# Eight last heads transposed by DMA, the last products one step later, and one low part moved ahead of the first rotation

## What is computed

```python
# part 1: x0 = x + einsum('bct,bcd->bdt', x, weights[subjects])      (32 x 32 weights per sequence)
# part 2: x0 + attention(x0)
q = rmsnorm(x0 @ Wq.T, q_norm_w)      # 32 heads of 128
k = rmsnorm(x0 @ Wk.T, k_norm_w)      # 8 heads of 128
v = x0 @ Wv.T                         # 8 heads of 128
q, k = rope(q, pos), rope(k, pos)
k_all = concat([k_cache[block_table], k])     # 16 pages of 32 keys, and 32 new keys
v_all = concat([v_cache[block_table], v])
scores = where(valid, q @ k_all * SCALE, -1e30)   # each key head serves four query heads
out = x0 + (softmax(scores) @ v_all) @ Wo.T
```

## Time and profile before

| | |
|---|---|
| median of three runs | 1012.82 us (1011.83 to 1014.14) |
| the profiled execution | 1012.16 us |
| its span, first to last instruction | 1010.1 us |
| busy: TensorE, VectorE, ScalarE, GpSimd | 96%, 81%, 73%, 54% |
| mean granted clock of TensorE | 0.997 |

### The profile page before, as it was taken

One profiled execution on the slowest core, in us unless ns is written; L12 is line 12 of the kernel. 1 busy time (PEld: TensorE's weight loads), 2 busy tenths in 40 slices (PEclk: granted clock), 3 DMA queues, 4 the chain that ended last, 5 costly groups with the idle time before them and its releaser, 6 DMA issues.

```text
span 1010.1 us, 24830 instructions
## 1 busy us (share of the span) xinstructions
PE 966.2 (96%) x8123; PEld 803.1 (80%) x8123; DVE 819.5 (81%) x1749; ACT 735.7 (73%) x2008; POOL 546.2 (54%) x715
## 2 busy tenths in 40 slices
PE   6899999999899999899999999999999999989998
PEld 4678888887677787688888888888888888878885
DVE  7789999999997689888877877777887787777770
ACT  5798999988774688777767767776776676766660
POOL 6565665565893068646644555454445545544540
PEclk9899999999999999999999999999999999999999
DMA  5799999989998989999999998998999998999940
GB/s 197 279 298 309 352 385 370 385 279 389 387 324 280 363 297 368 340 239 267 286 316 255 284 308 279 288 286 287 311 252 289 318 287 246 312 289 277 264 124 11
DMA packets 249903, 294.89 MB, mean 292 GB/s; under 512 B 79024, under 2 KB 206512, under 8 KB 247216
## 3 DMA queue, kind: packets, MB, share of 16 engines
q1 hardware_dynamic: 231088, 226.07, 74.9%
q0 software_dynamic: 18688, 67.25, 17.8%
HBM read 231.77 MB, written 46.27 MB: 275 GB/s over the span
## 4 chain that ended last, share of the span: by engine, by line
PE 70%; DVE 15%; ACT 5%; issue 5%; DMA 3%; POOL 2%; SPq 0%; DVEq 0%; ACTq 0%; POOLq 0%
PE ps_y L1491 16%; PE ps_proj L1491 15%; PE ps_o L1566 13%; PE ps_s L1529 8%; PE ps_s L1533 7%; PE ps_t L1540 7%; PE ps_rt L1661 2%; DMA w_nat<-in_L_cond_Wq 2%; DVE c_stage L1387 2%; DVE rot L1363 2%; DVE probs L1230 2%; DVE stage L1373 1%; PE ps_t L1548 1%; DVE rot L1355 1%; PE ps_o L1578 1%
## 5 line engine op out<-in xcount | busy, mean ns | idle before, releaser
L934 POOL TENSOR_SCALAR probs<-probs,recip 128x544 f32<-128x544 f32 (+1 forms) x256 | 162.7, 635 | 288.2 <-DVE recip L1238 280.5
L1008 ACT ACTIVATE probs<-probs,neg_max 128x544 f32<-128x544 f32 x256 | 191.0, 746 | 147.2 <-DVE neg_max L1230 143.9
L1230 DVE CUSTOM_DVE_ANT_0 probs<-ps_s,mask,row_scale 128x544 f32<-128x544 f32 x256 | 200.4, 783 | 64.2 <-PE ps_s L1533 60.9
L1566 PE MATMUL ps_o<-pt,vs 128*128 128x128 f16 x3072 | 213.5, 220 | 0.6 <-DMA vs<-v_pages,v_row 0.6
L1566 PEld LDWEIGHTS ps_o<-pt,vs 128*128 128x128 f16 x3072 | 192.7, 98 | 15.2 <-DMA vs<-v_pages,v_row 1.2
L887 POOL TENSOR_TENSOR roped<-rot 128x256 f32<-128x256 f32 x160 | 144.4, 923 | 82.6 <-DVE rot L1355 74.4
L1250 DVE SCALAR_TENSOR_TENSOR pt<-ps_t,pt 128x512 f16<-128x512 f32 x190 | 129.9, 684 | 48.9 <-ACT pt L1014 47.9
L1491 PE MATMUL ps_proj<-wt_hi,x0t_hi 128*128 128x512 f32 x384 | 159.7, 417 | 6.3 <-DVE x0t_lo L1188 5.8
L1491 PE MATMUL ps_y<-wo,ot_hi 128*128 128x512 f16 x512 | 153.6, 382 | 2.5 <-DVE ot_lo L1262 2.5
L1491 PE MATMUL ps_proj<-wt_hi,x0t_lo 128*128 128x512 f32 x384 | 151.4, 395 | 0.0
L1491 PE MATMUL ps_proj<-wt_lo,x0t_hi 128*128 128x512 f32 x384 | 150.6, 393 | 0.0
(11 more groups left out here) (156 smaller groups left out, 1657.0 us busy)
## 6 DMA issues: line engine op xcount, KB each, us to landing
kt<-k_pages_t SPq DMA_DIRECT2D x512, 128.0 KB
c_nat<-in_L_cond_k_cache SPq DMA_DIRECT2D x32, 512.0 KB, 6.2
q_t<-stage SPq DMA_DIRECT2D x64, 256.0 KB, 7.5
c_nat<-in_L_cond_v_cache SPq DMA_DIRECT2D x32, 512.0 KB, 7.0
qt<-q_t SPq DMA_DIRECT2D x32, 512.0 KB, 3.3
w_nat<-in_L_cond_Wq SPq DMA_DIRECT2D x8, 1024.0 KB, 8.7
k_pages_t<-c_stage SPq DMA_DIRECT2D x16, 512.0 KB, 5.6
c_nat<-in_L_cond_Wo SPq DMA_DIRECT2D x16, 512.0 KB, 7.5
```

The lines of the kernel that those rows point to most:

```text
L934: pool.tensor_scalar(part, part, col(recip, i), 1.0, ALU.mult, ALU.mult).then_inc(p_norm, 1)
L1008: act.activation(pr, pr, ACT.Exp, bias=col(neg_max, i), scale=-1.0, accum_out=col(row_sum, i)).then_inc(a_exp, 1)
L1230: dve.tensor_tensor_reduce(out=probs_of(i), in0=ps_s[:, score_cols(i):score_cols(i) + KEYS], in1=mask[(i // HK) % 2][:, mask_at(i):mask_at ...
L1566: ins = pe.matmul(ps_o[n % 2][:, jl * P:(jl + 1) * P], v[:, part, :], pt[pt_slot(i)][:, NCH * half + c, :], start=jl == 1 and c == 0 and k ...
```

## The change

1. `DMA_ALL = NP2 - HK = 248`: of the last sequence all eight heads are `by_dma`, so 249 to 251 and 253 to 255 beside 248 and 252. Their split rows lie in `kt[0]`, the keys of the sequence before, each head in a place of its own; rows_hi waits until the scores of head 247 are done.
2. For heads from 248 on, ACT does rows_hi(i + 2) behind exp(i + 3) and no longer ahead of t_hi(i), and DVE does row_recip(i + 2) behind masked_max(i + 3).
3. The products of the last group begin in step 257: eight, eight and 16.
4. DVE does `x_low(2)` ahead of the loop over units, so ahead of the first rotation.

```diff
+    DMA_ALL = NP2 - HK
     def by_dma(i):
-        return DMA_FIRST <= i < NP2 and i % HPC == 0
+        return DMA_FIRST <= i < NP2 and (i % HPC == 0 or i >= DMA_ALL)
...
-    def split_rows(i, part):
-        return rows[:, dma_no(i) % STAGED, part, :]
+    def split_rows(i):
+        if i < DMA_ALL:
+            return rows[:, dma_no(i) % STAGED]
+        return kt[B % 2][:, 0:HK * 2 * L].rearrange("p (n s f) -> p n s f", s=2, f=L)[:, i - DMA_ALL]
...
-    Y_LAST = {0: range(0, 4), 1: range(4, 10), 2: range(10, 16), 3: range(16, HQ)}
+    Y_LAST = {1: range(0, 8), 2: range(8, 16), 3: range(16, HQ)}
...
             for b in range(B):                                  # SP
-                turn_rows(HK * b + HPC)
+                for i in range(HK * b + 1, HK * b + HPC + 1):
+                    turn_rows(i)
...
-                turn_rows(HK * (b + 1))
+                for i in range(HK * b + HPC + 1, HK * (b + 1) + 1):
+                    turn_rows(i)
...
                 before = [h for h in range(i) if by_dma(h)][-STAGED:]      # rows_hi
-                if len(before) == STAGED:
+                if i >= DMA_ALL:
+                    act.wait_ge(t_qk, DMA_ALL)
+                elif len(before) == STAGED:
                     landed(act, before[0])
...
-                if by_dma(i + 2):                               # ACT, step i
+                if by_dma(i + 2) and i + 2 < DMA_ALL:
                     rows_hi(i + 2)
                 if i < NP2 and not by_dma(i):
                     t_hi(i)
                 if i + AHEAD < NP2:
                     exp(i + AHEAD)
+                if by_dma(i + 2) and i + 2 >= DMA_ALL:
+                    rows_hi(i + 2)
...
+            x_low(2)                                            # DVE, ahead of the units
             for u in range(NU):
                 c, g = units[u]
                 if c == 0:
-                    if 1 <= g and g + 1 < NG:
+                    if 2 <= g and g + 1 < NG:
                         x_low(g + 1)
...
-                if by_dma(i + 2):                               # DVE, step i
+                if by_dma(i + 2) and i + 2 < DMA_ALL:
                     row_recip(i + 2)
-                if late_new(i):
+                if late_new(i) and not by_dma(i):
                     t_lo(i)
                 if i + AHEAD < NP2:
                     masked_max(i + AHEAD)
-                if i + 2 < NP2 and not by_dma(i + 2):
+                if i + 2 < NP2 and (not by_dma(i + 2) or i + 2 >= DMA_ALL):
                     row_recip(i + 2)
```

More of the change, by code:

```diff
@@ L811, in turn_rows @@
                     pt_free(sp, i)
-                    sp.dma_start_transpose(pt[pt_slot(i)][:], rows[:, dma_no(i) % STAGED].rearrange("p s f -> p (s f)")
+                    sp.dma_start_transpose(pt[pt_slot(i)][:], split_rows(i).rearrange("p s f -> p (s f)")
                                            ).then_inc(d_pt[pt_slot(i)], 16)
             for b in range(B):
-                turn_rows(HK * b + HPC)
+                for i in range(HK * b + 1, HK * b + HPC + 1):
+                    turn_rows(i)
                 if b + 2 < B:
@@ L1020, in rows_hi @@
                 before = [h for h in range(i) if by_dma(h)][-STAGED:]
-                if len(before) == STAGED:
+                if i >= DMA_ALL:
+                    act.wait_ge(t_qk, DMA_ALL)
+                elif len(before) == STAGED:
                     landed(act, before[0])
-                act.activation(split_rows(i, 0), old_keys(i), ACT.Copy, scale=col(split_by, i)).then_inc(a_phi, 1)
+                act.activation(split_rows(i)[:, 0], old_keys(i), ACT.Copy, scale=col(split_by, i)).then_inc(a_phi, 1)
             def tn_hi(n):
@@ L1244, in rows_lo @@
                 dve.wait_ge(a_phi, dma_no(i + 1))
-                dve.scalar_tensor_tensor(split_rows(i, 1), old_keys(i), col(split_by, i), split_rows(i, 0),
+                dve.scalar_tensor_tensor(split_rows(i)[:, 1], old_keys(i), col(split_by, i), split_rows(i)[:, 0],
                                          ALU.mult, ALU.subtract).then_inc(v_plo, 1)
```

## The result

| | before | after |
|---|---|---|
| median us (runs) | 1012.86 (6) | 1018.94 (6) |
| lowest to highest us | 1011.27 to 1014.14 | 1017.96 to 1019.91 |
| profiled execution us, its span | 1012.16, 1010.1 | 1018.42, 1016.4 |
| mean granted clock of that execution | 0.997 | 0.996 |

The changed kernel takes 1.0061 of the time before, interval 1.0048 to 1.0074: 6.1 us more. The forecast was 1017.3.

The account below looks back on a forecast made before the run. TensorE, busy 96%, bounds the kernel; late heads would follow the ring's pace. 1012.16 − 2.6 (front) + 5.2 (tail) + 1.9 (clock) = 1016.7, with 0.66 for the median 1017.3; range 1012.3 to 1020.5.

Parts of the forecast that it names:

- The ring: Last heads: masked_max, exp, rows_hi, rows_lo, next masked_max wait in turn; 3.02 us a step against 2.37, five times.
- Rival (d): The ring does not bind, scores still set the pace, TensorE gets its 2.6 us: 1007.6; chance 0.10.
- (e): Rival: the ring binds by half, 2.7 us a step, tail +2.6, no change, 1012.8; chance 0.10.
- The entry: Where the ring begins, masked_max(250) comes 1.1 us late, bounds 0 and 1.6.
- The landing: Last head's DMA transpose lands 2.3 us after its issue, so weigh(255) starts at 989.3.
- Rival (c): DMA transposes land in 6.6 us and not 2.3, as eight follow each other: 1021.6; chance 0.05.
- The clock in the tail: TensorE, idle ahead of weigh(255), falls to half clock and loses 1.2 to 3.4 us, taken as 1.9.
- Rival (a): The ring binds but TensorE keeps its clock: 1015.4; chance 0.19.
- The low part: Front: x_low(2) moved ahead of the first rotation lets TensorE start the third and fourth tiles earlier: −2.6 us.
- Rival (b): The front's gain is lost by half clock in the fourth tile: 1019.9; chance 0.08.
- The products: Starting output products one step later removes a cover for the wait for weigh(255), worth at most 1 us.
- TensorE's 2.6 us of transposes: Six heads' transposes that TensorE no longer does turn into idle time, already counted in the tail's +5.2.

Follow-up runs that it names:

- e5: Kernel before, only its own DMA heads 248 and 252 in late order (rows_hi behind exp, row_recip behind masked_max): 1014.72 us, 1.0023.
- e4: Kernel before plus the six more DMA heads, with rows_hi ahead of exp and row_recip ahead of masked_max: 1013.15 us, 1.0017.
- e6: The whole change, but rows_hi ahead of exp and row_recip ahead of masked_max for all heads: 1012.84 us, 1.001.
- e3: The change with the old product list and x_low(2) where it was, so DMA heads and late order alone: 1018.66 us, 1.0076.
- e7: The changed kernel plus 26 unused transposes filling TensorE's waits in the last three steps ahead of weigh(255): 1017.73 us, 1.0052.
- e9: The changed kernel run again unaltered, beside its version with added transposes: 1017.65 us, 1.0058 of the kernel before.
- e10: The changed kernel with 26 unused TensorE transposes, the same kernel as e7 run again: 1017.05 us, 1.0046.
- e1: Kernel before with x_low(2) ahead of the first rotation and nothing else: 1009.72 us, 0.9988.
- e8: Kernel before with x_low(2) moved and the products one step later, no further DMA heads: 1010.71 us, 0.9984.
- e2: Kernel before with the last group's output products from step 257 on (8, 8, 16), nothing else: 1011.53 us, 1.0004.
- e12: e8 with ScalarE's first two key-cache scans behind the fourth tile's high part: 1009.34 us, 0.997.
- e11: The change in early order (rows_hi ahead of exp), with heads 254 and 255 left to TensorE: 1010.22 us, 0.9978.

## Why the prediction was right, and where it was off

**The ring: right, and shown.** Foretold were 3.02 us a step against 2.37; measured were 3.00 and 2.37. e5 makes the loss with the order alone, e4 and e6 take it away with the DMA heads still there. The table agrees: e4 against e3 has 3.6 us less of remaining span, and e5 has 2.6 more than before; in e5 the order closes at two steps only, so it shows the entry's cost twice and not the ring of five. Rival (d), that it does not bind, and (e), that it binds by half, are out.

**The entry: right.** 1.1 us foretold, 4.93 − 3.57 = 1.36 measured, twice more in e5.

**The landing: too small.** I took 2.3 us, the end of the packets in the earlier trace rows. The release of TensorE comes later: 3.06 us after the issue here, 3.04 in e7, 3.05 in e4. The last transpose is also not alone as that of the earlier trace rows was: the one ahead of it was issued 1.8 us before, and its own packets end 2.5 us after the issue. Windows of the changed kernel, issue at 985.25:

```profile
986.40:987.80 1.40, 1.26 (x12) 1.20 (x12) 1.04 (x3) 0.00 (x0) 0.00 (x0) 0.50 0.97 187
```

So from `masked_max(255)` to weigh(255) it is 8.0 us, not 7.3. Rival (c), a landing of 6.6 us, did not come about.

**The clock in the tail: right.** 1.9 us foretold. The profile gives 24.28 against the 22.3 that the prediction reckoned at full clock, 2.0; against the 22.49 that e7 took at full clock it is 1.8. The added transposes take no time in the tail: from `masked_max(255)` to weigh(255) it is 7.98 us in e9 and in e10. The 0.7 us more of remaining span in e10 lie within the 1.6 that the table books too much for such a tail. The mean spans of e9 and e10 differ by 1.5 us, the tails in the profiles by 1.7, and the medians by 0.6, of five and six runs. Rival (a), clock kept, is out for the change. The tail as a whole: 7.1 foretold, 8.0 in the profile. The difference, as rounded, is 0.3 at the entry, 0.7 at the landing, 0.1 in what lies behind it and −0.1 in the ring.

**The low part: mechanism right, size wrong.** This is the term that was mis-sized: −2.6 us, measured −1.2 (e1), −1.6 with the products (e8). Its step was "the third took 28.27 to 35.42": I took the 6.8 us of half clock in the one execution that I had as what the kernel has each time, and subtracted it from a median of others. From first to last low part of the front that execution took 40.05 us; e2, e3, e4 and e5, whose front is the same, took 38.56, 38.79, 38.77 and 37.25. Windows of e2, then of e5, the same stretch as in the earlier trace rows:

```profile
28.10:31.40 3.30, 2.95 (x8) 2.27 (x9) 2.76 (x5) 2.29 (x6) 2.37 (x5) 0.50 1.04 422
```

```profile
28.10:31.40 3.30, 2.95 (x15) 2.45 (x16) 2.74 (x5) 2.37 (x6) 2.56 (x5) 1.00 1.04 423
```

Half clock lasts 3.4 us in e2, e3 and e4, not 6.8, and in e5 there is none, behind the same idle gap of 2.8 us. The nine profiles with the low part moved have no half clock in the front and take 37.1 to 37.8 us from first to last low part (e1 37.52, the change 37.78). That is 1.2 and 0.9 less than the 38.7 of e2 to e4, and nothing less than e5. The table says the same in another way: the low part takes 1.9 us off the clock loss and nothing off the remaining span. So what moving it gave back was the clock. The Trainium skill (TensorE: Matmul & The Clock Gate, Part 1: The HAM clock gate) says half rate unless recent activity releases it; the rows agree that half clock stands behind idle time, but e5 shows that this gap doesn't always bring it. TensorE's idle time only moved to just ahead of the fourth tile: e1 has gaps of 1.38 and 1.36 us where it had one of 2.83. The scans that stand ahead of that tile are where e12 gained more (0.9984 to 0.997, intervals that overlap). Rival (b), half clock in the fourth tile, is out.

**The products: right in size, and their sign depends on the heads.** e2 lies at 1.0004. Its profile shows 28.1 us from `masked_max(255)` to the last product against 28.8, so without the DMA heads the edit wins 0.7 us that the medians don't show. With them it removes a cover, as foretold at up to 1 us: the same stretch is 28.74 in e4 and 29.87 in e6, which has the products later. So −1.6 and +7.7 make 6.1 with some luck, since the −1.6 holds a gain of the products that the changed kernel hasn't.

**TensorE's 2.6 us of transposes: idle time, as foretold.** Even in early order the heads give nothing (e4: 1.0017; e6: 1.001 where e8 has 0.9984). The forecast came out 1.6 us low (1017.3 against 1018.94): by the medians 1.0 of it is what e8 measures, −1.6 where −2.6 was foretold, and 0.6 what e3 measures, +7.7 where +7.1 was. The term that was mis-sized is the front's; the mechanism of the loss held.

**What stays open.** Of e4's 1.7 us the profile places 0.8 at the entry; the table gives about 0.9 to remaining span and 1.0 to the clock, and where that clock was lost differs from run to run. Why half clock comes behind a gap in one execution and not in the next stays open too. e11 does without the last two heads and is not told apart from e8; with all six it is 2.6 us more than e8 (e6), most of it in the wait for the last transpose, which e11 hasn't.

## What to carry to other kernels

Each engine here works in the order written for it, so putting a result's eviction behind the next step's work ties two steps together through both engines; add up the links once round and compare that with the pace, as 3.0 against 2.4 us a step here. A head moved off the bound engine is worth only what the engine then does earlier, and at the end of this kernel, where its wait for the last transfer begins, that was less than nothing: 2.6 us lost in the better of the two orders. Before a stretch of half clock in a profile is put into a sum, look at other executions of the same code, or at the mean clock of all runs: of five with the same gap one had twice the length of three others, and one had none.

## What the runs showed of the hardware that was not expected

- Half clock behind the same idle gap (2.82 to 2.84 us ahead of the third tile) lasted 6.8 us in the execution before, 3.4 in e2, e3 and e4, and did not come in e5. In the tail it lasted 6.8 us in the change and in e9, and 3.4 in e3.
- It also comes up in the body, in some executions. Near 901 us TensorE waits 2.35 to 2.36 us for GpSimd's `norm` in all 14 profiles; half clock follows in two of them (e4, e5; 3.4 us each) and not in the other twelve. Timeline of TensorE in e5, then windows:

```profile
901.26 1.06 PE L1542 MATMUL ps_t<-fixed,probs 128*128 128x128 f32 x4 [2.36 <-POOL probs L934]
```

```profile
895.00:901.00 6.00, 3.90 (x46) 3.29 (x44) 4.93 (x13) 4.34 (x10) 2.95 (x4) 1.00 0.89 312
901.40:904.70 3.30, 3.30 (x22) 2.87 (x22) 0.69 (x1) 0.60 (x1) 2.30 (x3) 0.50 0.94 300
```

  TensorE is busy for 3.9 of the 6 us ahead of it, up to that gap. Such stretches are part of the spread between runs of one kernel: of the 27 runs of before beside e1, clock and span go together with a correlation of −0.82.
- With no page loads beside it, the last transpose of 128x1024 fp16 by the DMA releases its waiter 3.04 to 3.06 us after its issue, in all seven profiles that have it, though in the changed kernel its packets were over after 2.5.
